# First layer: rows split by POOL and VectorE and turned by DMA, a fifth block of weights in single precision

## The reference

```python
# L0 attention: 32 heads of 16, one key and one value head shared by all
q = (hidden_states @ Wq).reshape(b, s, NUM_HEADS, HEAD_DIM)
kv = hidden_states @ Wkv
scores = jnp.einsum('bqhd,bkd->bhqk', q, k) * scale
scores = jnp.where(causal[None, None], scores + bias[None], -jnp.inf)   # ALiBi bias
attn = jax.nn.softmax(scores, axis=-1)
out = jnp.einsum('bhqk,bkd->bqhd', attn, v).reshape(b, s, h)
return out @ Wo
# L0 ffn: one dequantised matrix
out = jnp.einsum('bsi,oi->bso', x, W) + bias
```

## Time and profile before

| | us |
|---|---|
| median of 3 runs | 2198.66 |
| lowest, highest | 2198.51, 2199.24 |
| profiled execution | 2201.45 |
| its span, first to last instruction | 2199.3 |
| TensorE busy in the span | 2061.8 (94%) |
| VectorE busy | 1755.3 (80%) |
| ScalarE busy | 1387.8 (63%) |
| POOL busy | 950.2 (43%) |

### The profile page before, as it was taken

One profiled execution on the slowest core, in us unless ns is written; L12 is line 12 of the kernel. 1 busy time (PEld: TensorE's weight loads), 2 busy tenths in 40 slices (PEclk: granted clock), 3 DMA queues, 4 the chain that ended last, 5 costly groups with the idle time before them and its releaser, 6 DMA issues. The chain is left out here.

```text
span 2199.3 us, 48564 instructions
## 1 busy us (share of the span) xinstructions
PE 2061.8 (94%) x18563; PEld 1248.1 (57%) x18563; DVE 1755.3 (80%) x3692; ACT 1387.8 (63%) x3037; POOL 950.2 (43%) x902
## 2 busy tenths in 40 slices
PE   8798999898878899999999999999999999888998
PEld 3466666666434556656566565666666665534443
DVE  5799899998766787778878778777877877967665
ACT  3466665666456777777777777767777876661221
POOL 0188798879743323233333332332333323253221
PEclk9899999999879999999999999999999999999999
DMA  6110101101122453354354354444354443420001
GB/s 240 47 36 17 55 17 48 36 18 41 44 96 55 92 101 76 71 95 92 63 97 90 67 93 89 71 91 92 63 99 80 73 89 76 98 71 27 32 20 39
DMA packets 390214, 153.81 MB, mean 70 GB/s; under 512 B 358544, under 2 KB 369424, under 8 KB 387936
## 3 DMA queue, kind: packets, MB, share of 16 engines
q1 hardware_dynamic: 389984, 150.71, 31.5%
HBM read 48.69 MB, written 11.53 MB: 27 GB/s over the span
## 5 line engine op out<-in xcount | busy, mean ns | idle before, releaser
L1899 POOL TENSOR_TENSOR q_in_sbuf<-q_in_sbuf,sinq 128x512 f32<-128x512 f32 x128 | 162.6, 1271 | 720.1 <-ACT q_in_sbuf L2031 598.5
L2043 ACT ACTIVATE xp<-xp,nm 128x128 f32<-128x128 f32 (+3 forms) x512 | 281.3, 550 | 199.0 <-DVE nm L2126 199.0
L1925 PE MATMUL bank<-xT_hi,weights_and_hi 128*128 128x512 f16 x1280 | 383.0, 381 | 7.0 <-DVE yacc L2141 3.8
L872 ACT ACTIVATE weights_and_hi<-bank,unit 128x512 f32<-128x512 f32 x320 | 213.4, 687 | 152.3 <-PE bank L671 149.6
L2008 ACT ACTIVATE probs_hi<-xp,rl 128x128 f16<-128x128 f32 (+3 forms) x512 | 245.1, 550 | 68.2 <-DVE rl L2146 64.4
L2095 DVE SCALAR_TENSOR_TENSOR probs_lo<-xp,rl,probs_hi 128x128 f16<-128x128 f32 (+3 forms) x512 | 282.4, 612 | 0.0
L2103 DVE TENSOR_TENSOR q1T_lo<-qf,q1T_hi 128x512 f16<-128x512 f32 x128 | 88.4, 691 | 222.8 <-ACT q1T_hi L2022 222.8
L2126 DVE CUSTOM_DVE_ANT_0 xp<-bank,mask,cs 128x128 f32<-128x128 f32 (+3 forms) x512 | 250.3, 545 | 0.0
L1925 PE MATMUL bank<-xT_lo,weights_and_hi 128*128 128x512 f16 x640 | 243.6, 381 | 0.0
L564 POOL CAST weights_and_hi<-weights_and_hi 128x1024 f16<-128x1024 f32 (+1 forms) x192 | 198.4, 1053 | 85.9 <-ACT weights_and_hi L872 85.4
L1925 PE MATMUL bank<-p1T_hi,v_hi 128*128 128x128 f16 x1280 | 221.0, 219 | 2.6 <-DMA p1T_lo<-probs_lo 2.6
(11 more groups left out here) (311 smaller groups left out, 5498.2 us busy)
## 6 DMA issues: line engine op xcount, KB each, us to landing
weights_and_hi<-in_wq SPq DMA_DIRECT2D x8, 1024.0 KB, 6.0
raw_o<-in_wo SPq DMA_DIRECT2D x8, 1024.0 KB, 6.0
x_front<-in_x SPq DMA_DIRECT2D x5, 1024.0 KB, 6.1
q_stack<-q_hi SPq DMA_DIRECT2D x64, 64.0 KB, 2.6
wup<-in_wup SPq DMA_DIRECT2D x3, 1024.0 KB, 11.9
fused_scratch<-weights_and_hi SPq DMA_DIRECT2D x12, 256.0 KB, 2.5
xb<-in_x SPq DMA_DIRECT2D x3, 1024.0 KB, 5.2
x_scratch<-xb SPq DMA_DIRECT2D x3, 1024.0 KB, 4.3
```

The lines of the kernel that those rows point to most:

```text
L872: act.activation(px[:, p % 2, i, :], bank_of(("x", p, i))[:, :], ACT.Exp, scale=unit[:, 0:1]).then_inc(s_ed, 1)
L1899: pool.tensor_tensor(qs[:, i % 2, :], qs[:, i % 2, :], rope["sink" if u[0] == "k" else "sinq"][:, :], ALU.mult).then_inc(s_rot, 1)
L1925: ins = pe.matmul(out, lhs(a), rhs(c), start=(first and i == 0), stop=(last and i == 2))
L2043: ins = act.activation(x, x, ACT.Exp, scale=-1.0, bias=nm[:, m % 3, t:t + 1], accum_out=ls[:, m % 3, t:t + 1])
```

## The change

Turns of `n1`, `o`, `n2` and `n3`, except those after the last step, no longer use TensorE, ScalarE or a bank. POOL casts the tile's rows to half precision (`rows_hi`), VectorE subtracts the low half (`rows_lo`), both into a buffer of two places, and SP transposes each half by a DMA of 128x512 (`turn_rows`). Each turn has a number, and four semaphores in rotation count the DMAs. POOL casts the first two turns of a step at its end and a third at the start of the next; VectorE subtracts in the next step, the first two after its second `weights_lo`, a third after two more maxima; SP turns them at the head of the next step. The products that read turned rows wait for the DMAs. `o`, `y` and `f` move by a step in the table.

In `weigh_values` the fifth block of the weights is multiplied as it is, in single precision, with the values in single precision (`v_full`), which ScalarE copies once for each sequence. POOL's cast and subtraction of that block are gone.

```diff
+        rw = [sc.sb("rows_hi", [P, 2, S], F16), sc.sb("rows_lo", [P, 2, S], F16)]
+        vf = sc.sb("v_full", [P, 2, TT, EV])
-        BACK = {"load": 30, "o": (14, 18, 22, 25), "y": (26, 27, 28, 30), "n2": (36, 37), "f": (37, 38, 39, 40),
+        BACK = {"load": 30, "o": (13, 17, 21, 24), "y": (26, 28, 29, 30), "n2": (36, 37), "f": (38, 38, 39, 40),
...
+                def turn_rows(u):
+                    i, (kind, b, t) = turn_no[u], u
+                    sp.wait_ge(s_rl, i + 1)
+                    if i >= 4:
+                        sp.wait_ge(s_tp[i % 4], 32 * (i // 4))
...
+                    for half in range(2):
+                        sp.dma_start_transpose(transposed(u, half), rw[half][:, i % 2, :]).then_inc(s_tp[i % 4], 16)
...
                 for n in STEPS:
+                    for u in turns(n - 1):
+                        turn_rows(u)
                     b = at(n, FRONT["load"])
...
-                    for i, (c0, c1) in enumerate(((0, 2), (2, 4), (4, 5))):
+                    for c0, c1 in ((0, 2), (2, 4)):
                         pool.wait_ge(*emptied[("x", p, c1 - 1)])
                         pool.tensor_copy(ph[0][:, p % 2, c0:c1, :], px[:, p % 2, c0:c1, :]).then_inc(s_wh, 1)
-                    pool.wait_ge(s_wh, 3 * p + 3)
-                    pool.tensor_tensor(ph[1][:, p % 2, 4, :], px[:, p % 2, 4, :], ph[0][:, p % 2, 4, :],
-                                       ALU.subtract).then_inc(s_wc, 1)
...
+                def rows_hi(u):
+                    i, (rows, ready) = turn_no[u], rows_of(u)
+                    pool.wait_ge(*ready)
+                    if i >= 2:
+                        pool.wait_ge(s_rl, i - 1)
+                        pool.wait_ge(s_tp[(i - 2) % 4], 32 * ((i - 2) // 4 + 1))
+                    pool.tensor_copy(rw[0][:, i % 2, :].rearrange("p (k c) -> p k c", c=P), rows).then_inc(s_rh, 1)
+
                 for n in STEPS:
+                    for u in turns(n - 1)[2:]:
+                        rows_hi(u)
...
+                    for u in turns(n)[:2]:
+                        rows_hi(u)
...
+                                if i == 4:
+                                    ins = pe.matmul(out[:, at:at + EV], px[:, p % 2, i, c:c + P], vf[:, p // PAIRS % 2, j, :],
+                                                    start=False, stop=(j == t), skip_group_check=True)
+                                    continue
...
+                def rows_lo(u):
+                    i, (rows, _) = turn_no[u], rows_of(u)
+                    dve.wait_ge(s_rh, i + 1)
+                    if i >= 2:
+                        dve.wait_ge(s_tp[(i - 2) % 4], 32 * ((i - 2) // 4 + 1))
+                    hi, lo = (x[:, i % 2, :].rearrange("p (k c) -> p k c", c=P) for x in rw)
+                    dve.tensor_tensor(lo, rows, hi, ALU.subtract).then_inc(s_rl, 1)
...
                         weights_lo(n - X_LAG - 1, 1)
+                    for u in turns(n - 1)[:2]:
+                        rows_lo(u)
                     if 0 <= n < NP:
                         maximise(n, (2, 3))
+                    for u in turns(n - 1)[2:]:
+                        rows_lo(u)
```

More of the change, by code:

```diff
@@ L293, in layer0 @@
         s_ta = sc.sem("s_tail_added")
+        s_rh = sc.sem("s_rows_hi")
+        s_rl = sc.sem("s_rows_lo")
+        s_tp = [sc.sem(f"s_rows_turned{i}") for i in range(4)]
         s_tf = sc.sem("s_t_filled")
@@ L357, in offset @@
         def offset(kind, b, t):
-            late = {("f", LAST - 1, TT - 1): 41, ("o", LAST, TT - 1): 24}
+            late = {("f", LAST - 1, TT - 1): 41}
             return late.get((kind, b, t), BACK[kind][t])
@@ L374, in others, with turns @@
                 out.append(("V", at(n, FRONT["V"])))
+            return out
+        def turns(n):
+            out = []
             for kind, when in (("n1", FRONT["n1"]), ("n2", BACK["n2"]), ("n3", BACK["n3"])):
@@ L379, in others @@
                         out += [(kind, b, 2 * i), (kind, b, 2 * i + 1)]
-            out += [("o", b, t) for t in range(TT) for b in range(B) if n == PAIRS * b + offset("o", b, t)]
-            return out
+            return out + [("o", b, t) for t in range(TT) for b in range(B) if n == PAIRS * b + offset("o", b, t)]
+        turn_no = {u: i for i, u in enumerate(u for n in STEPS for u in turns(n))}
         fillings = {"s": [], "x": [], "rest": [], "end": []}
@@ L411, in layer0 @@
             filled[u], emptied[u] = (full, counted[full]), (empty, counted[full])
+        for u in turn_no:
+            filled[u] = (s_rl, turn_no[u] + 1)
         def bank_of(u):
@@ L455, in transposed, with rows_of, turned @@
             return bT[half][:, :, t * P:(t + 1) * P]
+        def rows_of(u):
+            kind, b, t = u
+            if kind == "o":
+                return on[:, :, t * P:(t + 1) * P], (s_on, PAIRS * b + GP * (t + 1))
+            rows = {"n1": xf, "n2": ya, "n3": yb}[kind]
+            return rows[:, t, :].rearrange("p (k c) -> p k c", c=P), (s_nm, TT * norm_no[kind, b] + t + 1)
+        def turned(u):
+            i = turn_no[u]
+            return s_tp[i % 4], 32 * (i // 4 + 1)
         def last_of(kind, b):
@@ L482, in stack_maxima @@
                                          mh[lo][16 * e:16 * (e + 1), g % 2, :]).then_inc(s_mr[g % 2], 16)
+                def turn_rows(u):
[3 more added lines that the diff above has]
+                        sp.wait_ge(s_tp[i % 4], 32 * (i // 4))
+                    if t == 0 and kind == "n1":
+                        sp.wait_ge(*filled[("q", GP * (b - 1) + 3)])
+                    if t == 0 and kind == "o" and b >= 1:
+                        sp.wait_ge(*last_of("y", b - 1))
+                    if t == 0 and kind == "n2" and b >= 1:
+                        sp.wait_ge(*last_of("f", b - 1))
+                    for half in range(2):
+                        sp.dma_start_transpose(transposed(u, half), rw[half][:, i % 2, :]).then_inc(s_tp[i % 4], 16)
                 def store_rows(b):
@@ L518, in _ @@
                         N1.load_others(sp)
+                for u in turns(STEPS[-1]):
+                    turn_rows(u)
+                for i in range(len(turn_no) - 4, len(turn_no)):
+                    sp.wait_ge(s_tp[i % 4], 32 * (i // 4 + 1))
                 store_rows(LAST - 1)
@@ L713, in ready_bank, with all_turned @@
                     if kind == "K" and b:
-                        pe.wait_ge(*emptied[("n1", b, TT - 1)])
+                        all_turned("n1", b)
                     elif kind == "q" and b >= GP:
-                        pe.wait_ge(*emptied[("n1", b // GP, TT - 1)])
+                        all_turned("n1", b // GP)
                     elif kind == "y":
-                        pe.wait_ge(*emptied[("o", b, TT - 1)])
+                        all_turned("o", b)
                     elif kind == "f":
-                        pe.wait_ge(*emptied[("n2", b, u[2])])
+                        pe.wait_ge(*(emptied[("n2", b, u[2])] if b == LAST else turned(("n2", b, u[2]))))
                     return out
+                def all_turned(kind, b):
+                    for t in range(TT):
+                        pe.wait_ge(*turned((kind, b, t)))
                 def half(u, i):
@@ L758, in fill @@
                         N1.spread(pe, take(u))
-                    elif kind == "o":
-                        transpose4(u, on[:, :, u[2] * P:(u[2] + 1) * P], (s_on, PAIRS * b + GP * (u[2] + 1)))
-                    else:
-                        rows = yl if (kind, b) == ("n3", LAST) else {"n1": xf, "n2": ya, "n3": yb}[kind]
-                        if b == LAST and kind != "n1":
+                    else:
+                        rows = yl if (kind, b) == ("n3", LAST) else {"n2": ya, "n3": yb}[kind]
+                        if b == LAST:
                             ready = (s_tn, tail_no[1 if kind == "n2" else 3, u[2]])
@@ L816, in hi4 @@
                     kind, b, t = u
-                    if t == 0 and kind == "n1":
-                        act.wait_ge(*filled[("q", GP * (b - 1) + 3)])
-                    if t == 0 and kind == "o" and b >= 1:
-                        act.wait_ge(*last_of("y", b - 1))
                     if t == 0 and kind == "n2" and b >= 1:
@@ L1039, in evacuate @@
                     kind, b = u[0], u[1]
[L1040 to L1042 removed]
+                    if kind == "K":
                         join_keys(u)
```

28 lines of the change are left out of this document (14 added, 14 removed).

## The result

| | before | after |
|---|---|---|
| median, us | 2198.95 (2198.51 to 2199.27, 4 runs) | 2316.93 (2315.68 to 2320.43, 4 runs) |
| ratio, 95% interval | | 1.0536 (1.0523 to 1.0548) |
| profiled span, us | 2199.3 | 2314.8 |
| TensorE's mean granted clock | 0.978 | 0.944 |

The change costs 118 us. The forecast was 2253, in a range of 2203 to 2285: slower was right, and the size was less than half of what came.

What follows compares the result with a forecast made beforehand. The prediction took TensorE and VectorE, both nearly full, as the bound. Late maxima 48, engine work 5, third-turn waits 6, layer end 5, less 9 for the tail made +55 us: 2253 us, range 2203 to 2285.

Steps and rivals of the forecast that it cites:

- The chain of the late maxima: At eight of sixteen groups SP's transposes delay the maxima TensorE needs: waits of 64.7 us, +48 us after recovery.
- a: Time SP takes to issue one transposing DMA of four blocks: put at 0.9 us, bounds 0.59 and 1.34.
- T0: End of the step's first row subtraction on VectorE, the earliest moment for transposes: 319.40 us at step 36.
- Rival 2: Freeing POOL decides: VectorE and POOL stop disturbing each other, about 2173 us; new subtractions can be blocked too; chance 0.13.
- The recovery: TensorE catches up between late groups in its idle time: 2.1 us each, 17 us in eight.
- rival 3: Ten-block issue and landing, single-precision matmuls at 0.36 us, lower TensorE clock after long waits: +94, about 2293 us; chance 0.07.
- The scaling of the issue by blocks: On SP, a transposing DMA's excess issue time over a plain one grows with its blocks, giving 0.9 us for four.
- The work of TensorE and VectorE, +5: Middle of TensorE's added 16 us (single precision less turns) and VectorE's 7 us relief: +5 us, -17 to +23.
- The end: At the layer's end the last turn stands behind SP's loads, +5 us; a shorter POOL-bound tail gives -9.
- The gain of 9 from POOL's rest: After the last scores POOL is the bound; without the fifth block five steps save 1.7 us each: -9 us.
- The two third-turn waits, +6: At steps 37 and 53, VectorE waits 2.9 us each for the third turn's cast: +6 us, 3 to 8.
- Rival 1: Late maxima are mostly swallowed, TensorE recovering 5 us per wait, not 2.1: +5 to +30, about 2218 us; chance 0.12.

Runs made afterwards that it cites:

- e1: Changed kernel with SP issuing a step's maxima ahead of its transposes instead of after them: 2260.2 us, ratio 1.0279 to the kernel before.
- e4: Kernel before, with SP issuing the maxima at seven groups only after VectorE's last maximum of the following step: 2242.3 us, ratio 1.02.
- e7: Changed kernel with 30 to 56 dummy matmuls on TensorE ahead of each of the eight waits: 2300.6 us, ratio 1.0464.
- e12: Changed kernel with maxima first, next layer's loads behind the last turn, three row places, and plain DMAs instead of transposing ones: 2246.8 us, ratio 1.0221.
- e14: Changed kernel with maxima first, loads behind the last turn, three row places, and a step's first two row subtractions before its first two maxima: 2237.1 us.
- e16: Changed kernel with only the subtraction of the rows moved ahead of the first two maxima, transposes still ahead of the maxima: 2291.5 us, ratio 1.0416.
- e2: Kernel before with only the fifth block of the weights in single precision, turns still on TensorE: 2207.5 us, ratio 1.0045.
- e15: e14 with four overwritten dummy transposes on TensorE added for each turned tile: 2243.7 us, ratio 1.0208.
- e13: e2 plus two transposing DMAs of 128x512 for each turn, into a block nobody reads: 2219.7 us, ratio 1.0089.

## Why the prediction was wrong

**The chain of the late maxima: right.** The eight groups, the cause on SP and the form of the waits were as forecast. The waits at steps 48, 52 and 24 had been put at 7.5, 7.5 and 11.1 us, and came as 7.56, 7.51 and 11.76. Others were longer, 10.47 against 6.35 at step 36. Of those 4.1 us, 1.6 are mostly the issue: from the first transpose to the exponents it was 8.8 us, not 7.25, because a was 1.24 us and not 0.9. The other 2.5 are the start: TensorE came 1.6 us ahead of the first transpose, where T0 had been put 0.9 before TensorE. Part of it is the first `rows_lo` itself. It lasted 1.52 us (356.72 to 358.24), not the 0.60 that was put in, beside a cast of POOL (least, median and most ns of the two at this place, then the cast):

```profile
L1086 DVE TENSOR_TENSOR rows_lo<-ya,rows_hi x2: 679/1098/1517, 356.7 to 358.2; 128x512 f16<-128x512 f32 x2
```

```profile
356.53 1.17 POOL L609 CAST weights_and_hi<-weights_and_hi 128x1024 f16<-128x1024 f32 x1 [0.82 <-ACT weights_and_hi L930]
```

All 48 took 0.67 to 1.74 us. Rival 2 had named such a stretching, and the sum left it out.

**Its price: mis-sized by 9, and three errors in it partly cancel.** The waits summed to 79.4 us, not 64.7, just beyond the upper bound of 77.9. The term was 57 us, not 48, and in the bounds of 38 to 61. The recovery, which I put at 17 us in eight groups, was real: 25 us between the marks in the changed kernel against e1, though only 7 in e4 with its shorter waits. What the sum had at nothing is the clock. Between the marks TensorE's busy time was 12.1 us longer than in e1 and 7.6 longer in e4 than before, and filling the waits gave 16 us back (e7). That was rival 3's mechanism, to which I gave 7 in 100, and it belonged in the forecast. That longer waits and the clock on one side and more recovery on the other left only 9 us is in part luck.

**The scaling of the issue by blocks: wrong.** Interpolating between 0.59 and 1.34 us by the number of blocks gave 0.9; 128x512 took 1.24, nearly what 128x1280 took, so the kind of DMA decides here and not its size. The landing, 2.4 to 2.5 us, was below my 3.0. The Trainium skill ("Advanced Engine Details and Errata", X-Bar Transpose) says that such DMAs are as fast as regular ones. That holds here for the landing (2.1 to 2.4 us for the plain ones of e12, 2.4 to 2.5 for these) and not for the issue (0.6 against 1.2 to 1.27).

**Everything but the maxima: the step that failed most.** I had 5 + 6 + 5 - 9 = +7 us for the rest. It was 61. The step that failed is that a turn by DMA was booked as relief of TensorE alone, and the way of the turned rows, outside the maxima's DMAs, at nothing.

- *The turns' own way.* A turn by DMA is a chain of cast, subtraction, two issues and a landing, in which VectorE's part stands in the middle of its step. Products wait for turned rows, maxima for the subtraction. I had followed it into the maxima's DMAs and no further. The late place alone costs 22 to 25 us (e14, e16), the rest of the turns some 30 more (e14 less e2). Those 30 have the relief of TensorE in them already, which is worth 6.6 us (e15) and not 21.
- *The work of TensorE and VectorE, +5: near, by luck.* Measured it is 9 (e2) less 6.6 (e15), some 2 us, since the cost of single precision and the worth of the relief were both put too high. The matmul itself cost what was forecast, 0.22 us, and VectorE's `weights_lo` fell from 1.409 to 1.357 us, 6.7 us in 128, as booked. By e2's profile TensorE has 38 us more work between the marks and 18 us less idle time, so it costs 20 us there, against 9 by the medians.
- *The end.* For the stretch from step 64 to the second layer I forecast 5 - 9 = -4 us beside the eighth late group. 21 came, 8.2 of them the maxima's, so 13 stand against the -4. The wait for the last turn was 8.07 us instead of 5. The gain of 9 from POOL's rest was 2.3 in e2. And TensorE's granted clock in this stretch fell from 0.79 to 0.64 (below).

The end of the steps, e2 and e14, then before and after, as windows from `m_lo` of step 64 to the second layer's first matmul:

```profile
560.50:614.10 53.60, 50.06 (x570) 35.28 (x570) 37.27 (x54) 27.95 (x51) 29.26 (x31) 0.81 0.17 46
```

```profile
571.30:637.60 66.30, 56.23 (x541) 36.01 (x541) 40.19 (x55) 22.44 (x40) 38.96 (x40) 0.64 0.36 78
```

```profile
540.00:596.00 56.00, 46.46 (x599) 29.56 (x597) 39.39 (x54) 26.88 (x49) 43.80 (x43) 0.79 0.16 44
```

```profile
639.00:715.90 76.90, 54.56 (x537) 34.70 (x534) 42.19 (x57) 22.58 (x41) 37.52 (x40) 0.64 0.36 70
```

In both kernels that turn by DMA TensorE issues fewer instructions here and is busy for longer, at 0.64 of its clock. The long wait of step 64 isn't what keeps it low: in e7, where dummies fill that wait, the clock was up for some 7 us behind it and then at the lower level until 676 all the same (granted clock 0.50 from 656 to 676).

**The two third-turn waits, +6.** All of VectorE's waits for POOL's casts of the rows summed to 8.6 us in the changed kernel up to 690 us, 2.75 of them at step 40, with 5.4 more at the last turn. No run prices those of steps 37 and 53 by themselves. The third place, which is to take such waits away, brought nothing once the maxima were first.

**The rivals.** Rival 1 (recovery decides) is refuted by e1 and e4, where the late maxima cost 57 and 44 us, and rival 2 (POOL's relief decides) by the result and e2. Rival 3 named the clock and gave 2293, but reached it with a cost of single precision that didn't come, so even it lacked the turns' own cost.

**What stays open.** The rest of the turns by DMA, some 30 us by medians or 24 by profiles, isn't taken apart by a run. Half of it lies at the end of the steps. Between the marks TensorE is busy 8 us less than in e2 and idles 19 more, at a clock of 0.94 against 0.96. The waits that grew are those for the maxima of the scores, 21.0 us against 6.8, and for turned rows, 6.0 against none (e14 between the marks):

```profile
PE bank L716 <- DVE mx L1146: 14.3, 19, 1.6
PE bank L716 <- DVE mx L1144: 6.2, 9, 1.9
PE bank L698 <- DMA heads_T_lo<-rows_lo: 6.0, 2, 3.0
```

Together they grew by some 20 us, about the idle time; no run takes them away. That the low clock at the end comes of TensorE's short gaps is argued from the rows, and no run held TensorE busy through the whole of it. No version beat the kernel before.

## What to carry to other kernels

Before moving work off a full engine, follow the data and not only the engine's time: here 21 us of TensorE's work were exchanged for a chain through four queues, and the place of one link in VectorE's step cost 22 to 25 us, where the work was worth 6.6. On a queue that issues in order, put what an engine waits for every time ahead of what can wait, and give a new waiting instruction the whole list of what stands behind it. Price each wait of a full TensorE at about its length (41 us more of them cost 42 in e4, 63 cost 50 in the changed kernel): what is recovered elsewhere, the lower clock behind the wait takes back in whole or in part.

## What the runs showed of the hardware that I had not expected

- A transposing DMA of 128x512 takes SP 1.19 to 1.27 us to issue, and one of 128x1280 takes 1.34: nearly the same. Plain ones of 128x512 take 0.6.
- Two such DMAs more for each turn doubled the DMA share (0.10 to 0.22) between the marks, and the profiled executions of e2 and e13 have the same length and the same busy times there.
- A subtraction of 128x512 on VectorE lasted 0.67 to 1.74 us. At step 36 it took 1.52 where a cast of POOL had begun 0.2 us earlier, and the next one took 0.68.
- Behind the first seven waits of 7 to 13 us TensorE ran at the lower level for 8 to 10 us. Dummy matmuls in the wait kept it at the upper one behind seven of eight; behind the one where they ended 3.4 us early it ran at the lower one.
